# One transformer decoder layer: in self-attention, queries taken by VectorE, transposes copied ahead of projections, forget-gate columns in two parts

## What is computed

```
xn = layer_norm(x)                       # over 256 columns
q, k, v, p, y = split(xn @ W_in.T + b_in)    # 512, 512, 512, 512 and 16 columns
k = (1 - smear) * k + smear * k_previous_row      # per head
pos = cumsum(sigmoid(y))                 # one forget gate per head and row
scores = (q/s) @ (k/s).T / sqrt(32) + causal - (pos_i - pos_j)
o = softmax(scores) @ v                  # 16 heads of 32 columns
out = layer_norm((silu(p) * o) @ W_out.T);  x1 = layer_norm(x + out)
```

## Time and profile before

| what | us |
|---|---|
| median of 3 runs (2684.51 to 2691.44) | 2685.38 |
| profiled execution | 2680.88 |
| its span | 2679.0 |
| busy: TensorE / VectorE / ScalarE / GpSimd | 2382.6 / 1817.7 / 1727.8 / 936.7 |

### The profile page before, as it was taken

How to read it: one execution, slowest core, us unless ns; L and a number is a source line. 1 busy time by engine, 2 the same in 40 slices (tenths; PEclk the granted TensorE clock), 3 DMA queues, 4 the chain that set the end, 5 groups by cost and what they waited for, 6 DMA issues and landing times. The chain is left out here.

```text
span 2679.0 us, 61019 instructions
## 1 busy us (share of the span) xinstructions
PE 2382.6 (89%) x17865; PEld 1973.1 (74%) x17865; DVE 1817.7 (68%) x5239; ACT 1727.8 (64%) x4347; POOL 936.7 (35%) x983
## 2 busy tenths in 40 slices
PE   4888888885799999999999999999999379999991
PEld 3777777774677777777777777777776379999991
DVE  4766767665567666766677666766676268787776
ACT  3888888885466666666566656666566156676662
POOL 3454444444432233223332233223331134444434
PEclk8999999998899999999999999999999689999995
DMA  5644555453000000000000000000000166767766
GB/s 124 176 112 113 125 129 112 110 117 86 24 10 16 17 17 1 16 17 17 9 9 16 17 17 1 16 17 17 9 8 9 61 216 230 244 230 229 244 219 196
DMA packets 160229, 224.40 MB, mean 84 GB/s; under 512 B 33872, under 2 KB 127696, under 8 KB 159568
## 3 DMA queue, kind: packets, MB, share of 16 engines
q1 hardware_dynamic: 149040, 201.88, 26.8%
q0 software_dynamic: 9664, 20.53, 2.3%
q10 hardware_dynamic: 1376, 0.54, 0.1%
HBM read 140.15 MB, written 24.01 MB: 61 GB/s over the span
## 5 line engine op out<-in xcount | busy, mean ns | idle before, releaser
L1517 DVE CUSTOM_DVE_ANT_0 x_prob<-x_score,x_mask_add 128x512 f32<-128x512 f32 x512 | 348.1, 682 | 282.7 <-PE x_score L1748 226.7
L1320 ACT ACTIVATE x_prob<-x_prob,x_low 128x512 f32<-128x512 f32 x512 | 366.5, 718 | 199.4 <-DVE x_low L1517 195.6
L1326 ACT COPY x_pt<-x_ptb 128x512 f32<-128x512 f32 x512 | 272.9, 584 | 244.3 <-PE x_ptb L1760 243.4
L1241 POOL TENSOR_TENSOR x_k_lo<-x_whole,x_k_hi 128x512 fp32r<-128x512 f32 x128 | 165.9, 1296 | 413.7 <-ACT x_k_hi L1366 411.3
L1528 DVE TENSOR_SCALAR x_prob<-x_prob,x_rden 128x512 f32<-128x512 f32 x512 | 272.9, 574 | 0.6
L1760 PE MATMUL x_ptb<-ident,x_prob 128*128 128x128 f32 x2048 | 267.7, 274 | 2.6 <-PEq L1791 2.3
L484 ACT ACTIVATE prob<-prob,low 128x128 f32<-128x128 f32 (+1 forms) x512 | 233.5, 468 | 54.9 <-DVE low L727 53.8
L1777 PE MATMUL x_av<-x_pt,x_vx 128*64 128x256 f32 x2048 | 249.3, 385 | 0.8 <-ACT x_pt L1326 0.8
L1760 PEld LDWEIGHTS x_ptb<-ident,x_prob 128*128 128x128 f32 x2048 | 230.6, 141 | 14.3 <-issue 11.6
L1497 DVE COPY x_whole<-x_proj 128x512 f32<-128x512 f32 x192 | 130.8, 687 | 130.5 <-PE x_proj L1681 128.5
L1777 PEld LDWEIGHTS x_av<-x_pt,x_vx 128*64 128x64 f32 x2048 | 135.9, 136 | 100.1 <-issue 44.8
(11 more groups left out here) (276 smaller groups left out, 7246.7 us busy)
## 6 DMA issues: line engine op xcount, KB each, us to landing
w_s<-w SPq DMA_DIRECT2D x156, 512.0 KB
k_parts<-k_hi SPq DMA_DIRECT2D x128, 128.0 KB, 2.4
q_parts<-q_hi SPq DMA_DIRECT2D x128, 128.0 KB, 2.4
k_parts<-pos_parts SPq DMA_DIRECT2D x128, 64.0 KB, 2.4
k_parts<-k_lo SPq DMA_DIRECT2D x64, 128.0 KB, 2.4
q_parts<-q_lo SPq DMA_DIRECT2D x64, 128.0 KB, 2.4
w_s<-expert_rows SPq DMA_DIRECT2D x16, 512.0 KB, 4.7
b_s<-b SPq DMA_DIRECT2D x39, 128.0 KB
```

Source lines behind the costliest of these rows:

```text
L1241: pool.tensor_tensor(part_of(n, q_lo, k_lo), whole_of(n), part_of(n, q_hi, k_hi).bitcast(F32), ALU.subtract).then_inc(low_ready.sem, 1)
L1320: nc.scalar.activation(slot, slot, ACT.Exp, bias=low[:, u:u + 1], scale=-1.0, accum_out=den[:, u:u + 1]).then_inc(exp_ready.sem, 1)
L1326: nc.scalar.copy(pt[:, u % PX_RING, :], ptb[u % 2][:, :]).then_inc(pt_taken[u % 2].sem, 1)
L1517: dve.tensor_tensor_reduce(prob[:, u % PROB_RING, :], score[u % 2][:, :], mask_add[:, :], -X_SCALE, 3.0e38, ALU.add, ALU.min, low[:, u:u + ...
```

## The change

It does these things, all in `self_phase`:
- VectorE takes the queries (`take_q`: scale and bias, PSUM to q_t), in units 8 and 9; ScalarE makes q_hi by a rounding copy of q_t (`high_q`) in units 9 and 10; GpSimd's `low_q` waits for q_hi_ready.
- ScalarE's `take_transposed` stands ahead of the parts of each unit instead of behind them.
- The forget-gate columns win_y are split in a high and a low part; `project_y` uses `project_parts`, waits for xn_lo, and moves from the end of unit 2 to the front of unit 3, ahead of the first key chunk. `take_y` moves from unit 3 to unit 4.
- VectorE's parts are placed anew: `x_stats(b + 1)` from unit 10 to 4, `forget_gates` from 4 to 6, `centred` from 6 to 7, `silu` from 8 to 11, `place_pos` from 9 to 10, `residual_sum` from 11 to 10, and in unit 14 `gate` stands ahead of `half_p`.

```diff
--- before.py
+++ after.py
@@ -134,7 +134,9 @@
         win_s = wkv_s
         win_hi = sb("win_hi", [P, KC, 4 * D_EXP], F32R)
         win_lo = sb("win_lo", [P, KC, 4 * D_EXP], F32R)
-        win_y = sb("win_y", [P, KC, W_COLS - 4 * D_EXP])
+        win_y = sb("win_y", [P, KC, HEADS])
+        win_y_hi = sb("win_y_hi", [P, KC, HEADS], F32R)
+        win_y_lo = sb("win_y_lo", [P, KC, HEADS], F32R)
         wo = sb("wo", [P, EC, D])
         smls = sb("smls", [P, 2 * EC])
         by = sb("by", [HEADS, 1])
@@ -227,6 +229,7 @@
         proj_taken = [sig(f"proj_taken{i}", FILLS // 2) for i in range(2)]
         k_prev_ready, k_hi_ready = sig("k_prev_ready", 2), sig("k_hi_ready", 2)
         pos_steps, p_half_ready = sig("pos_steps", 4), sig("p_half_ready", 2)
+        q_hi_ready = sig("q_hi_ready", 2)
         q_split, k_split = sig("q_split", 2), sig("k_split", 2)
         out_used = sig("out_used", 1)
         silu_ready = sig("silu_ready", 1, 0)
@@ -239,7 +242,7 @@
         pt_filled = sig("pt_filled", HEADS)
         pt_taken = [sig(f"pt_taken{i}", HEADS // 2) for i in range(2)]
         av_done, gated = sig("av_done", HPC), sig("gated", HPC)
-        N_CONSTS, N_VCONSTS, N_IN, N_LATE = 10, 8 + KC, 16 * (9 + 2 * EC), 16 * 4
+        N_CONSTS, N_VCONSTS, N_IN, N_LATE = 10, 9 + KC, 16 * (9 + 2 * EC), 16 * 4
         xn_hi_ready, xn_split = sig("xn_hi_ready", 1), sig("xn_split", 1)
 
         def gate_columns(w, k):
@@ -375,8 +378,7 @@
 
                 for n in range(2):
                     m = slice(2 * n, 2 * n + 2)
-                    f = QP + n
-                    pool.wait_ge(proj_taken[f % 2].sem, proj_taken[f % 2].at(b, f // 2 + 1))
+                    pool.wait_ge(q_hi_ready.sem, q_hi_ready.at(b, n + 1))
                     pool.tensor_tensor(q_lo[:, m, :], q_t[:, m, :], q_hi[:, m, :].bitcast(F32), ALU.subtract).then_inc(q_split.sem, 1)
 
             def low_k(b):
@@ -467,6 +469,7 @@
             for k in range(KC):
                 nc.scalar.copy(win_hi[:, k, 0:3 * D_EXP], win_s[:, k, 0:3 * D_EXP])
                 nc.scalar.copy(gate_columns(win_hi, k), gate_columns_of(win_s, k)).then_inc(consts_a, 1)
+            nc.scalar.copy(win_y_hi[:], win_y[:]).then_inc(consts_a, 1)
             act.wait_ge(consts_v, N_VCONSTS)
 
             def taken(ins, f):
@@ -502,17 +505,12 @@
                 filled(b, YP)
                 taken(nc.scalar.activation(gate_tanh[:], proj[YP % 2][0:HEADS, 0:S], ACT.Tanh, bias=half_by[:, 0:1], scale=0.5), YP)
 
-            def take_q(b, n, i):
+            def high_q(b, n):
                 f = QP + n
-                if n == 0 and i == 0:
+                if n == 0:
                     act.wait_ge(q_split.sem, q_split.at(b - 1, 2))
-                filled(b, f)
-                m = 2 * n + i
-                for dst in (q_t, q_hi):
-                    ins = nc.scalar.activation(dst[:, m, :], proj[f % 2][:, i * S:(i + 1) * S], ACT.Identity,
-                                               bias=q_bias[:, m:m + 1], scale=q_scale[:, m:m + 1])
-                if i == 1:
-                    taken(ins, f)
+                act.wait_ge(proj_taken[f % 2].sem, proj_taken[f % 2].at(b, f // 2 + 1))
+                nc.scalar.copy(q_hi[:, 2 * n:2 * n + 2, :], q_t[:, 2 * n:2 * n + 2, :]).then_inc(q_hi_ready.sem, 1)
 
             def smear_k(b, n):
                 f = KP + n
@@ -555,8 +553,7 @@
                     smear_k(b, n)
                     high_k(b, n)
                 for n in range(2):
-                    for i in range(2):
-                        take_q(b, n, i)
+                    high_q(b, n)
                 for n in range(2):
                     tanh_p(b, n)
 
@@ -564,19 +561,18 @@
             for n, s in enumerate(pt_taken):
                 act.sem_inc(s.sem, (HEADS - COPY_LAG + 1 - n) // 2)
             projections(-1)
-            steps = {1: [take_xt], 3: [take_y], 4: [lambda b: smear_k(b, 0)], 5: [lambda b: smear_k(b, 1)], 6: [lambda b: high_k(b, 0)],
-                     7: [lambda b: high_k(b, 1), lambda b: take_q(b, 0, 0)], 8: [lambda b: take_q(b, 0, 1)], 9: [lambda b: take_q(b, 1, 0)],
-                     10: [lambda b: take_q(b, 1, 1), take_output(0)], 11: [take_output(1)], 13: [lambda b: tanh_p(b, 0)],
-                     14: [lambda b: tanh_p(b, 1)]}
+            steps = {1: [take_xt], 4: [take_y, lambda b: smear_k(b, 0)], 5: [lambda b: smear_k(b, 1)], 6: [lambda b: high_k(b, 0)],
+                     7: [lambda b: high_k(b, 1)], 9: [lambda b: high_q(b, 0)], 10: [lambda b: high_q(b, 1), take_output(0)],
+                     11: [take_output(1)], 13: [lambda b: tanh_p(b, 0)], 14: [lambda b: tanh_p(b, 1)]}
             outputs = {10: [take_output(0)], 11: [take_output(1)]}
 
             def one_pass(b, parts):
 
                 for i in range(HEADS):
                     exps(b, i)
+                    take_transposed(*unit(b, i - COPY_LAG))
                     for part in parts.get(i, ()):
                         part(b)
-                    take_transposed(*unit(b, i - COPY_LAG))
 
             with act.Fori(0, B - 1) as b:
                 one_pass(b, steps)
@@ -632,6 +628,8 @@
                 dve.tensor_tensor(win_lo[:, k, 0:3 * D_EXP], win_s[:, k, 0:3 * D_EXP], win_hi[:, k, 0:3 * D_EXP].bitcast(F32), ALU.subtract)
                 dve.tensor_tensor(gate_columns(win_lo, k), gate_columns_of(win_s, k), gate_columns(win_hi, k).bitcast(F32),
                                   ALU.subtract).then_inc(consts_v, 1)
+            dve.wait_ge(consts_a, 2 + KC + 1)
+            dve.tensor_tensor(win_y_lo[:], win_y[:], win_y_hi[:].bitcast(F32), ALU.subtract).then_inc(consts_v, 1)
             for s in (x1_stored, score_taken):
                 dve.sem_inc(s.sem, s.per)
             for s in (rden_known, rden_ready):
@@ -685,6 +683,17 @@
                                                    op0=ALU.mult, op1=ALU.add)
                 taken(ins, f)
 
+            def take_q(b, n):
+                f = QP + n
+                if n == 0:
+                    dve.wait_ge(q_split.sem, q_split.at(b - 1, 2))
+                filled(b, f)
+                for i in range(2):
+                    m = 2 * n + i
+                    ins = dve.tensor_scalar(q_t[:, m, :], proj[f % 2][:, i * S:(i + 1) * S],
+                                            q_scale[:, m:m + 1], q_bias[:, m:m + 1], ALU.mult, ALU.add)
+                taken(ins, f)
+
             def half_p(b, n):
                 f = PP + n
                 filled(b, f)
@@ -772,25 +781,29 @@
             for n in range(2):
                 take_k(-1, n)
             for n in range(2):
+                take_q(-1, n)
+            for n in range(2):
                 half_p(-1, n)
             x_stats(0)
             steps = {0: [lambda b: one_over_sums(b - 1, 3), lambda b: take_v(b - 1, 0)],
                      1: [lambda b: widen(b - 1, 3), lambda b: gate(b - 1, 2)],
                      2: [lambda b: take_v(b - 1, 1)],
                      3: [lambda b: out_stats(b - 1)],
-                     4: [lambda b: one_over_sums(b, 0), forget_gates],
+                     4: [lambda b: one_over_sums(b, 0), lambda b: x_stats(b + 1)],
                      5: [lambda b: widen(b, 0), lambda b: gate(b - 1, 3)],
-                     6: [lambda b: take_k(b, 0), lambda b: centred(b - 1)],
-                     7: [lambda b: take_k(b, 1)],
-                     8: [lambda b: one_over_sums(b, 1), silu],
-                     9: [lambda b: widen(b, 1), place_pos],
-                     10: [lambda b: x_stats(b + 1)],
-                     11: [lambda b: residual_sum(b - 1)],
+                     6: [lambda b: take_k(b, 0), forget_gates],
+                     7: [lambda b: take_k(b, 1), lambda b: centred(b - 1)],
+                     8: [lambda b: one_over_sums(b, 1), lambda b: take_q(b, 0)],
+                     9: [lambda b: widen(b, 1), lambda b: take_q(b, 1)],
+                     10: [lambda b: residual_sum(b - 1), place_pos],
+                     11: [silu],
                      12: [lambda b: one_over_sums(b, 2), lambda b: residual_stats(b - 1)],
                      13: [lambda b: widen(b, 2), lambda b: half_p(b, 0)],
-                     14: [lambda b: half_p(b, 1), lambda b: gate(b, 0)],
+                     14: [lambda b: gate(b, 0), lambda b: half_p(b, 1)],
                      15: [lambda b: gate(b, 1)]}
-            last = {**steps, 4: steps[4][:1], 6: steps[6][1:], 7: [], 9: steps[9][:1], 10: [], 13: steps[13][:1], 14: steps[14][1:]}
+            last = {**steps, 6: [], 7: steps[7][1:], 10: steps[10][:1], 14: steps[14][:1]}
+            for i in (4, 8, 9, 13):
+                last[i] = steps[i][:1]
 
             def one_pass(b, parts):
 
@@ -857,14 +870,13 @@
 
             def project_y(b):
                 bk_ = free(b, YP)
-                in_sbuf(b, XT)
-                full(project(bk_[0:HEADS, 0:S], lambda k: win_y[:, k, :], lambda k: xn_t[:, k, :], KC))
```

(9 more changed lines are left out.)

## The result

| kernel | median us (lowest to highest) | runs | profiled execution, us | span, us |
|---|---|---|---|---|
| before | 2686.22 (2684.51 to 2691.44) | 4 | 2680.88 | 2679.0 |
| after | 2787.36 (2779.05 to 2791.29) | 4 | 2791.29 | 2789.5 |

The change makes the kernel slower: the ratio is 1.0372, 95% interval 1.0355 to 1.0390. That is 101 us more; the prediction was 59 us more, with 2765 us as the upper end of its range. The sign and the ring are as predicted, its size is not. The profiled execution of after is the slowest of its four. One execution of experiment 6 (4847 us) and one of the kernel before beside experiments 9 and 10 (7592 us) ran in a slow state and are left out of the medians and ratios.

A forecast was written before the change was run, and what follows sets the result against it. A ring from x_raw's landing through VectorE and SP's queue bounds each pass: 39.3 us, 40.6 with clock loss, against 37.56. The last pass starts at 676.2 us instead of 617.3, +59 us: 2744 us, range 2715 to 2765.

The forecast's parts named there:

- the ring: x_raw lands, x_stats, VectorE's units 5 to 10, place_pos, SP's DMA list, x_raw again: 39.3 us, 40.6 with clock loss; 0.67.
- The waits at units 9 and 10 for a copy and for a query: TensorE's waits of 1.16 us behind take_q and 1.20 us for take_q's second bank would go.
- L: Start of x_stats in a pass, zero point of the ring's times; the last was forecast at 649.1 us.
- SP's 3.3 and 19.96 us and the landing: SP's five k_parts DMAs 3.3 us, then 19.85 us to x_raw's issue, 2.7 us to its landing.
- take_q(1) 0.8, masked 10 0.56, residual_sum 0.85, place_pos 0.7: L + 13.35: VectorE's instructions from masked 9 to place_pos, ending 13.35 us after x_stats starts, before clock loss.
- The upper bound of 41.5 us: Longest pass allowed: clock loss of twice 1.2 us, the lines at half clock lasting longer.
- 15 x 0.098: TensorE's clock loss behind the idle stretch: 15 matmuls at half clock, 1.5 us a pass, less 0.2 us.
- Rival 2: The ring is longer, 42 us or more, GpSimd's q_lo or a loaded DMA queue ending last: 2764 us and up; 0.07.
- the signs: Expected in the profile: x_raw waits near 6 us each pass, TensorE's longest before scores 7 and q0, x_raw 40.6 us apart.
- Net so far: 2.4 us faster in a pass: All parts before the x_stats move: 2.7 us saved on waits less 0.3 us for later keys.
- y starts some 1.35 us after the point where the transposes start today: Forget-gate projection waiting for xn_lo on TensorE; keys 0.27 us later than in a full-clock pass.
- The 2.7 us that I had for the copies and queries: Gain a pass from removing the waits at units 9 and 10 with small gaps: 1.35 + 1.34 us.

The follow-up runs named there:

- experiment 6: Changed kernel with x_stats back in unit 10, y in fp32 at the end of unit 2 and take_y in unit 3: 2666.61 us, 0.9919 of before.
- experiment 9: Kernel before with only the forget-gate columns split, y at the front of unit 3 behind xn_lo: 2688.48 us, 1.0002 of before.
- experiment 10: Kernel before with only copies ahead of the parts on ScalarE and queries taken by VectorE in units 8 and 9: 2646.34 us, 0.9843 of before.
- experiment 1: Changed kernel with x_stats(b + 1) put back in unit 10 behind place_pos, the rest kept: 2700.34 us, 1.0052 of before.
- experiment 2: Kernel before with only x_stats(b + 1) moved from unit 10 to unit 4: 2722.29 us, 1.0136 of before.
- experiment 5: Changed kernel with SP issuing x_raw ahead of the last group's eight spreading DMAs, one load added: 2707.04 us, 1.0069 of before.
- Experiment 4: Changed kernel with one added wait, GpSimd starting q_lo only when place_pos is done: 2747.95 us, 1.0221 of before.
- Experiment 3: Changed kernel with place_pos ahead of residual_sum in unit 10: 2736.90 us, 1.0179 of before.
- experiment 8: Kernel before with only queries taken by VectorE in units 8 and 9, rounded by ScalarE in 9 and 10: 2650.52 us, 0.9863.

## Why the prediction was right in its sign and short in its size

*The ring.* This was right, and is shown by experiments 1, 2 and 5: the load that VectorE waits for, the place of that wait at the head of units 5 to 10, SP's list as the way back. The waits at units 9 and 10 for a copy and for a query are gone, as said. The forecast links that hold within 0.3 us are take_k(0) (L + 4.23 for 4.2), the start of the queries, SP's 3.3 and 19.96 us and the landing.

*The step that failed* is "take_q(1) 0.8, masked 10 0.56, residual_sum 0.85, place_pos 0.7: L + 13.35". I priced residual_sum and place_pos by their time beside an idle GpSimd, and counted high_q(1) and q_lo, which the change puts in just these microseconds, only as work that had to be ready for SP. They took 1.97 and 0.27 + 1.52 us. Against 0.88 + 0.27 + 0.41 in experiment 4, that is 2.2 us in the ring. The upper bound of 41.5 us held more clock loss, but nothing for this. Experiment 4 isolates it: 2.4 us a pass come back when GpSimd leaves the overlap, and nothing else is changed. Experiment 3 agrees with it (2.6 us, residual_sum's own time among them). The rest of the 2.97 us a pass (43.57 for 40.6) is the clock, whose "15 x 0.098" was a stretch of 3.2 us taken from the prologue and is 4.7 us here (431.79 to about 436.5), for 0.5 us more up to scores 9, and 0.3 us of wake, list and landing. No run changes the clock alone.

*Rival 2*, "The ring is longer than I think" ("GpSimd's q_lo or a loaded DMA queue ends last"), 42 us or more, had the right length and the wrong mechanism: SP waited for place_pos, and GpSimd did its harm by being beside it. Of the signs, the longest waits before scores 7 and before the queries came as said. TensorE was also held by xn_lo, 2.2 us a pass, without being what sets the pass.

*"Net so far: 2.4 us faster in a pass"* was wrong too, and the ring hid it. Experiment 1 is 13 us slower than before. "y starts some 1.35 us after the point where the transposes start today" missed the clock: the 2.16 us wait stands close behind where the removed 2.27 us one stood, and the half clock comes with it as it did with that one (experiment 6: 2.4 us a pass). The rest is likely the overlap of q_lo again: in experiment 1 residual_sum and place_pos take 2.2 us more, and scores 12 wait 0.98 us for VectorE. No run takes the overlap away there. The 2.7 us that I had for the copies and queries came out in number, by luck: experiment 10 gains 43 us in 15 passes, 2.9 us each, but at the same clock a pass is only 1.7 us shorter (34.6 for 36.3). The rest is half clock that went from ten passes, which the term did not hold.

*The sum*, in profiled executions: 110.5 us measured for 59. The last L lies 39.7 us later than forecast (14 x 2.97, less 1.9 for a first load that landed in 6.7 us), the way from it to the last pass's first scores is 29.4 us for 27.1, the last pass takes 4.5 us more up to its output projection (32.8 us for 28.3), and what follows it 5.1 us more. In the last pass the windows show the clock at half from 731 to 736 us:

```profile
731.00:736.00 5.00, 5.00 (x32) 3.73 (x31) 1.94 (x11) 3.08 (x14) 0.00 (x0) 0.50 0.01 3
```

The 5.1 us behind it lie within the scatter: in the twelve profiled executions of this study that part, which no edit touches, takes between 2031.3 and 2038.5 us, and before and after lie near the two ends. The medians lie 101 us apart, not 110.

## What to carry to other kernels

When a load is consumed earlier, follow its issue back through the queue to the engine that releases it: if the way leads through the consumer's own list, the wait closes a ring, and where the ring is longer than the pass, its length is the new time of a pass. Price each instruction on such a ring by what the other engines do in the same microseconds, GpSimd's tensor operations beside VectorE's two-input ones in SBUF above all, and put what releases a long queue ahead of everything that nobody waits for. Compare passes at the same granted clock before you give a gain to a wait. A change in many parts can hold a gain: here two of its parts are worth 1.6% and the others take 5.3% of before back.

## What the hardware showed

- VectorE operations with two inputs in SBUF stand still while GpSimd subtracts 128x512 tiles in SBUF: the 16x256 subtraction took 1.52 us instead of 0.41 and ended 0.28 us behind GpSimd's, two 128x256 operations 1.97 us instead of 0.88. The Trainium skill (SBUF — State Buffer, Who interferes with whom) states that such a pair contends over a shared read interface, and its Summary: rules for kernel authors that the one that starts second is blocked whole. The trace agrees: place_pos's subtraction started 0.03 us behind GpSimd's, and the second half of residual_sum some 0.04 us behind (an estimate: 441.08 + half of 0.88, for 441.48). In experiment 3 GpSimd came second, 0.09 us behind place_pos's 0.41 us, and it was GpSimd that took longer:

```profile
338.71 1.47 POOL L382 TENSOR_TENSOR q_lo<-q_t,q_hi 128x512 fp32r<-128x512 f32 x1 [4.19 <-ACT q_hi L513]
```

- Beside a GpSimd operation on 128x2 elements silu, also with two inputs in SBUF, took its usual 1.22 us (in the changed kernel it started at 445.39, within 444.97 to 445.69).

- A VectorE copy with one input in SBUF stood still as well: in experiment 1 rden_wide took 1.37 us instead of 0.29 when it started 0.06 us behind GpSimd's addition:

```profile
372.61 1.37 DVE L748 COPY rden_wide<-rden 128x256 f32<-128x256 f32 x1
```

```profile
372.55 1.29 POOL L394 TENSOR_TENSOR x_again<-x_again,row 128x512 f32<-128x512 f32 x1
```

- Operations whose first input comes from PSUM showed no such loss. In experiment 1 scaled_silu (av from PSUM, x_pt from SBUF) took its usual 0.41 us inside another of these GpSimd additions (at 333.78, within 333.67 to 335.01), and the masking its usual 0.28 and 0.42 us inside a GpSimd operation with one tensor input. VectorE and then GpSimd:

```profile
350.49 0.28 DVE L734 CUSTOM_DVE_ANT_0 prob<-score,causal 128x128 f32<-128x128 f32 x1
...
350.70 0.42 DVE L736 CUSTOM_DVE_ANT_0 prob<-score,causal 128x256 f32<-128x256 f32 x1
```

```profile
350.16 2.74 POOL L414 TENSOR_SCALAR zx<-x_raw,mv,rstd 128x256 f32<-128x256 f32 x2 [0.22 <-POOL rstd L375]
```

- How long TensorE's matmuls ran at half clock behind a wait did not follow the length of the wait: 3.2 us behind 3.16 us in the prologue of before, 4.7 us behind 3.03 and 1.74 us in the changed kernel, 5.9 us behind 2.16 us in experiment 1. Nor did the same waits always bring it: the two windows of experiment 8 above hold the same waits of TensorE (2.8 us for copies, the longest 2.3, and 0.4 us for take_k), one at 1.00 and the other at 0.95 and 1.55 us longer. What decides it no run here shows.
